# Cross-attention on one core: the side work of TensorE put behind the value products, and the accumulators turned before the last key read

## The reference

```python
Q = relu(queries @ Wq + bq); K = relu(keys @ Wk + bk); V = relu(values @ Wv + bv)   # keys = values = ctx
scores = einsum('hbqd,hbkd->hbqk', Qh, Kh) * (1 / sqrt(8))
scores = where(key_mask == 0, -2**32 + 1, scores)
attn = softmax(scores, axis=-1) * q_mask
out = einsum('hbqk,hbkd->hbqd', attn, Vh)  # heads put side by side
return out + queries
```

## Time and profile before

| | |
|---|---|
| Time of 3 runs | median 357.49 us (357.31 to 357.93) |
| Profiled execution: its own time | 357.66 us |
| Its span, first to last instruction | 355.8 us |
| TensorE busy | 346.1 us (97%) |
| ScalarE busy | 299.1 us (84%) |
| VectorE busy | 234.6 us (66%) |
| Granted TensorE clock, mean | 0.997 |
| Chain that ended last | PE 88%, DVE 4%, DMA 3%, issue 2% |

### The profile page before, as it was taken

One profiled execution on the slowest core, in us unless ns is written; L12 is line 12 of the kernel. 1 busy time (PEld: TensorE's weight loads), 2 busy tenths in 40 slices (PEclk: granted clock), 3 DMA queues, 4 the chain that ended last, 5 costly groups with the idle time before them and its releaser, 6 DMA issues.

```text
span 355.8 us, 16795 instructions
## 1 busy us (share of the span) xinstructions
PE 346.1 (97%) x6698; PEld 232.7 (65%) x6698; DVE 234.6 (66%) x777; ACT 299.1 (84%) x394; POOL 4.5 (1%) x28
## 2 busy tenths in 40 slices
PE   7999999999999999999999999999999999999993
PEld 4666676766767676676767667676666757676662
DVE  5789596875939577593957759395775939579211
ACT  1587788888888988888898888889888888989993
POOL 5000000000000000000000000000000000000000
PEclk9999999999999999999999999999999999999998
DMA  6778766767835746384573638457363845537000
GB/s 192 265 247 281 227 230 201 294 203 245 302 95 208 214 149 194 93 318 105 206 215 134 210 89 315 112 194 226 131 213 89 304 123 189 158 129 219 9 11 6
DMA packets 41809, 65.35 MB, mean 184 GB/s; under 512 B 28213, under 2 KB 30901, under 8 KB 41781
## 3 DMA queue, kind: packets, MB, share of 16 engines
q1 hardware_dynamic: 40562, 64.15, 55.9%
q10 hardware_dynamic: 1218, 0.79, 0.8%
HBM read 13.73 MB, written 0.82 MB: 41 GB/s over the span
## 4 chain that ended last, share of the span: by engine, by line
PE 88%; DVE 4%; DMA 3%; issue 2%; ACTq 1%; ACT 1%; SPq 0%; DVEq 0%
PE psum L685 35%; PE psum L661 28%; PE psum L605 12%; PE psum L596 12%; DMA bq_sb<-in_bq 2%; DMA k_parts<-k_low 1%; DVE v_biased L924 1%; DVE k_cent L900 1%; DVE values L934 1%; ACT probs L559 0%; DVE k_low L905 0%; DVE k_high L900 0%; PE psum L625 0%; PE psum L776 0%; SPq L357 0%
## 5 line engine op out<-in xcount | busy, mean ns | idle before, releaser
L559 ACT ACTIVATE probs<-psum 121x800 f32<-121x800 f32 x384 | 293.2, 841 | 39.1 <-PE psum L661 39.1
L685 PE MATMUL psum<-probs,values 121*17 121x200 f32 x3072 | 153.4, 333 | 0.0
L661 PEld LDWEIGHTS psum<-query_bd,k_parts 64*121 64x121 f32 x1536 | 91.8, 181 | 45.2 <-issue 38.6
L685 PEld LDWEIGHTS psum<-probs,values 121*17 121x17 f32 x3072 | 87.0, 97 | 50.3 <-issue 20.3
L661 PE MATMUL psum<-query_bd,k_parts 64*121 64x200 f32 x1536 | 115.6, 281 | 0.4 <-ACT probs L559 0.2
L881 DVE TENSOR_SCALAR_CACHE_REDUCE k_raw<-psum,bk_sb 128x361 f32<-128x361 f32 (+2 forms) x63 | 37.6, 598 | 79.2 <-PE psum L596 78.9
L605 PE MATMUL psum<-wv_sb,keyT 128*32 128x129 f32 (+1 forms) x1536 | 54.5, 277 | 0.6 <-DVE v_biased L924 0.4
L596 PE MATMUL psum<-keyT,wk_mixed 128*32 128x361 f32 (+2 forms) x504 | 52.0, 487 | 0.1
L934 DVE TENSOR_SCALAR values<-v_biased,keep 121x128 f32<-121x128 f32 x192 | 43.4, 282 | 6.2
L605 PEld LDWEIGHTS psum<-wv_sb,keyT 128*32 128x32 f32 (+1 forms) x1536 | 38.2, 108 | 8.0 <-DVE v_biased L924 2.0
L924 DVE TENSOR_TENSOR v_biased<-psum,bv_sb 121x384 f32<-121x384 f32 x64 | 35.0, 547 | 0.0
(11 more groups left out here) (74 smaller groups left out, 65.4 us busy)
## 6 DMA issues: line engine op xcount, KB each, us to landing
k_parts<-k_high SPq DMA_DIRECT2D x30, 722.0 KB, 4.7
k_parts<-k_low SPq DMA_DIRECT2D x30, 722.0 KB, 5.4
keyT<-in_ctxT SPq DMA_DIRECT2D x15, 722.0 KB, 4.4
query_rep<-late_high SPq DMA_DIRECT2D x2, 600.0 KB, 3.7
query_rep<-late_low SPq DMA_DIRECT2D x2, 600.0 KB, 4.2
residual<-in_x SPq DMA_DIRECT2D x64, 12.5 KB
out<-residual SPq DMA_DIRECT2D x60, 12.5 KB
k_parts<-k_high SPq DMA_DIRECT2D x2, 359.0 KB, 3.8
```

Source lines behind the costliest of these rows:

```text
L559: nc.scalar.activation(probs[0:KTILE, u % PROB_SLOTS], scores_ps[0:KTILE, u % SCORE_SLOTS, :, 0:QCOLS], ACT.Exp, scale=SCALE).then_inc(pro ...
L661: mm = nc.tensor.matmul(scores_ps[0:KTILE, u % SCORE_SLOTS, j, n * TCOLS:(n + 1) * TCOLS], k_parts[rows, parity, t, kt * KTILE:(kt + 1) * ...
L685: mm = nc.tensor.matmul(spans[c * VCOLS:c * VCOLS + VUSED, half, :, :, 0:SPAN], values[0:KTILE, parity, kt, half * HALF_PAIRS + c, 0:VUSED ...
```

## The change

In the cycles from batch 1 on, the side work moves from between the scores and the value products to behind the value products. In VectorE's list the turning of the accumulators moves from `split_keys`, behind the last key piece and its maximum, to a place ahead of the read of the last key piece. In batch 0 only VectorE's list changes, where the turning comes ahead of the maximum of the keys of batch 2. The two checks of the last batch keep their place in the code of the cycle, which is now behind the value products.

```diff
@@ TensorE, batch @@
                     for u in units:
                         next_scores(u + LEAD)
+                    for u in units:
+                        value_products(b, parity, u)
                     k, ahead = SIDE_WORK[cycle]
                     if not last and (keys or ahead == NEXT):
                         prepare(b + ahead, (parity + ahead) % 2, k, used)
...
                         count_batches()
-                    for u in units:
-                        value_products(b, parity, u)
@@ VectorE @@
             def split_keys(b, used):
                 max_keys(b, used)
-                turn_outputs(b - 2)
                 dve.wait_ge(k_replicated, 16 * SLOTS * b)
...
                 read_rows(turn_of("rows"))
+                turn_outputs(0)
                 split_keys(2, turn_of("rows") + 1)
...
                     for c in range(KPARTS):
+                        if c == KPARTS - 1:
+                            turn_outputs(b)
                         read_keys(b + 2, c, used + c)
```

## The result

The changed kernel takes 356.47 us (median of 9 runs, 355.74 to 356.81); the kernel before, on the same chip, takes 357.58 us. The ratio is 0.9957, with a 95% interval from 0.9948 to 0.9967. A second, later comparison of the same two kernels gave 0.995 (0.9937 to 0.9963), 356.09 us. So the change makes the kernel 0.4 to 0.5% faster. Forecast were 355.6 us (-0.5%) and a range of 354.8 to 357.3; the profiled execution took 356.63 us with a span of 354.8, at a mean granted clock of 0.995.

What follows compares the result with a forecast made beforehand. TensorE was taken to set the pace, with ScalarE some 12% behind, until 325.34 us. Cycle -1.7, waits -0.40 and one stall +0.16 sum to -1.9 us: a median of 355.6 us, range 354.8 to 357.3.

Steps and rivals of the forecast that it cites:

- rival A: TensorE's order of work is free, only waits change: -0.24 us, giving 357.25 us; chance 0.22.
- Part 1: TensorE's loop cycles: new order saves 0.025 us per key cycle, 0.012 per value cycle; 2.0 us in all, taken as 1.7.
- V to the next S with W between them: TensorE, value products to next scores with side work between: 1.737 us with keys, 1.795 with values, from batch 0.
- V to W: TensorE, start of value products to start of side work behind them: 1.01 to 1.02 us.
- W to S: TensorE, start of side work to start of next scores: 0.72 us with keys, 0.78 with values.
- S to V: TensorE, start of scores to start of value products: taken as 0.815 us; 0.83 would cut the gain to 0.4.
- Part 2: Second value piece's wait for VectorE's first value read, in batches 4, 6, 8, 10, 12: goes, saving 0.40 us.
- Part 3: Batch ends: value products wait for turned accumulators only at batch 0's end, +0.16 us once; elsewhere 0.5 us of room.
- Part 4: Exponentials and the last batch's first check: no cost, put at 0 with 0.1 us either way.
- Rival B: First value products of batches 2 to 14 wait 0.25 us for late accumulators: slower, 358.9 us; chance 0.06.
- Rival C: Larger gain in TensorE's cycle, cheaper mode change behind side work, scores to value products 0.80 us: 353.6 us; chance 0.07.

## Why the prediction was right

The direction and the mechanism held, the size roughly: forecast -1.9 us, measured -1.1 in the first comparison (357.58 to 356.47) and -1.8 in the second (357.87 to 356.09). The time alone would not have decided: 356.47 us lies 0.87 from the forecast and 0.78 from rival A (357.25), and both lie in the range. The cycles decide.

**Part 1, the cycle (forecast -1.7, measured -1.13): right in kind, mis-sized.** This is the term that was off. The step that failed is the carrying over of batch 0: "V to the next S with W between them" was to be 1.737 us with keys and 1.795 with values, and is 1.749 and 1.802. Most of that is in V to W, 1.027 us instead of the 1.017 of batch 0; 0.003 us with keys is the rounding of the rows (the three samples are 1.740 before rounding); W to S is 0.722 and 0.775, as forecast. In batch 0 these value products stood behind a side piece, and four of their weight loads had been made under it. Now they stand behind the scores, and all 24 come with them. The kernel with the side piece in between shows that a side piece right behind the scores pays 0.02 us, and batch 14 of the kernel before that value products pay some 0.01 us there. The gain of a cycle is the one less the other: 0.015 us with keys, 0.007 with values. The forecast counted the first and not the second, though it took its samples from the very place where they differ. One of them even had it: behind the query projection (25.81 us, 128x128 tiles) V to W is 1.03 us, and that was the sample of 1.80 us with values, taken as undisturbed. S to V, on which the bounds hung, came at 0.812 us, at the good end.

**Part 2, the five waits (forecast -0.40, trace -0.41): right.** No value piece waits in the loop; the room reckoned as 0.8 us is 0.91. The kernel with `k_cent` late in the even batches shows the same -0.4 alone.

**Part 3, the turned accumulators: the room right, the one stall there in the second trace and put down to the wrong cause in the first.** The transpose starts 1.27 us after the last value products (forecast 1.33) and the next ones find 0.57 us of room after its end, where 0.5 was said. That it would stall by over 1 us left behind the maximum is shown by the kernel with the old list: 1.2 to 1.6 us in each of 13 batches. At the end of batch 0 the forecast was +0.16 for the transpose. The second trace of the changed kernel has just that, +0.14 behind the transpose. The first has +0.21 for ScalarE's slots: with a side piece so small a TensorE cycle of 2.32 us is hardly longer than three exponentials there (6 in 4.60 us), if its scores are not held up. The prediction, which took 2.21 us from the last batches for the limit, missed this second way, and since kernels with the old order have that stall too, it belongs to neither order. That the first comparison came near 0.16 was luck.

**Part 4, the rest (forecast 0 within 0.1): right.** From the fifth cycle of batch 14 to the issue of the last store it is 27.12 us where it was 27.13. Outside the sum lie 0.25 us of the start and 0.06 behind that store, in which nothing was changed.

**What the prediction wanted to see.** The cycles, forecast at 2.55 and 2.61 us, are 2.56 and 2.615; rival A had 2.58 and 2.62. One thing was plainly wrong: VectorE's waits for key pieces should have stayed near 79 us and are 54.2, because the transpose takes one in four of them. It has no part in the sum.

**Rival A, only the waits change (357.25 us)**, falls: that kernel was run and gives 0.999, against 0.9957 and 0.995. With it falls the reading by which the changes of tiles are merely counted: the count is the same in both orders and the order has a price of its own, if a small one. The change itself does cost the same behind either, as that reading says: 0.11 us more to the scores than to work with the same tiles, behind value products (1.13 against 1.017) and behind a key piece (0.722 against 0.610). **Rival B** didn't occur, but it is what happens with VectorE's old list, 4.6% slower. **Rival C** wanted 0.80 us from S to V and a cheaper change behind W; neither was there, by the same numbers.

## What to carry to other kernels

When the order of one engine's work is changed, the engines that read its results must have their lists changed with it: here either half alone cost 3.5 to 4.6%, the two together gained 0.4%. A step's price read from one place of a profile holds at another only if what stands right before it is the same too; look for such a sample before a hundredth of a microsecond is multiplied by 108. And compare starts: what a profile names as the cause of idle time changed from one name to another here, 24 us of it, with no change in the distance.

## What the runs showed of the hardware

A change between scores and value products on TensorE is dear, and this was the greatest surprise: 0.175 us behind scores (64-row tiles) and 0.13 us behind value products (128x32 tiles), 0.305 us for the pair, some 12% of a cycle. Between two kinds of work with the same tiles it was 0.01 us. The Trainium skill ("TensorEngine Tiling (Array Packing)", Key Properties) says that a change of tiling mode drains the array; the runs agree that a change costs, and give it a size. How much of it is the array running empty and how much the first weight loads, which then come with nothing beside them, they don't separate; the scores also have another number format in the kernel (F32R). A kernel that has fewer changes of this kind, longer runs of either, is what this price points to; score slots in PSUM stand in the way here, and it was not tried.

VectorE stood still once for 1.9 to 2.5 us in eleven of the twelve traces, always in the first batch behind its hardware loop and within two entries of its list around the end of the first key read, and for 4.54 us in the one with 24 instructions put in ahead, where the place moved by 24. It cost nothing where it fell into a wait, 1.5 us where TensorE needed what stood behind it, and 5.9 us in the longest case, 2.4 of them by the lower clock that followed. The traces show a fetch beside it. The profile counts transfers of the kind "instruction"; on their queue 14 there is none from about 103 us on until the stop, in any trace, and one of 8 KB falls in the stop or at its start in each of them. For the long stop, the stretch from 302.1 to 306.5 us:

```profile
q14 instruction: 1, 0.01, 0.4%
```

That one starts at 304.84 us, 2.8 us into the stop; in the kernel before it starts 0.4 us into it (306.86). Whose instructions it carries is not named. The Trainium skill ("Runtime: NRT & Kernel Launch", Instruction fetch mechanics) says that instructions are fetched in blocks, and that a taken branch to a place outside the blocks at hand stalls the fetch. The fetch beside the stop and the place that moves with the list agree with blocks. A taken branch doesn't stand there: in the kernel before, 43 instructions and 12 us of plain list lie between the branch that ends the loop and the stop. So the likely reading is a fetch that comes late; that is not shown.
